# Causal attention of 4 batches: the row maxima of a batch are taken among the units of the batch before it

## The chip, the cores and the metric

One core of a Trainium2 chip runs the whole program, a decoder of several layers. The metric is the device time of one execution in microseconds; the median of three runs is given. The engines are TensorE (PE in the rows; PEld is its weight load), VectorE (DVE), ScalarE (ACT), GpSimd (POOL) and SyncE (SP). Each runs its own queue in order and waits on semaphores; only TensorE writes the eight banks of PSUM with matmuls, and VectorE and ScalarE read them.

## What is computed

The change lies in one of twelve layers, a causal self-attention over `x` of 4 batches (B) x 512 positions (S) x 128, with 16 heads of 8:

```python
q = split_heads(x @ Wq + bq)
k = split_heads(x @ Wk + bk)
v = split_heads(x @ Wv + bv)
att = jnp.einsum('bhtd,bhsd->bhts', q, k) * (1.0 / math.sqrt(Dh))
causal = jnp.tril(jnp.ones((T, T), dtype=bool))
att = jnp.where(causal[None, None], att, -jnp.inf)
att = jax.nn.softmax(att, axis=-1)
o = jnp.einsum('bhts,bhsd->bhtd', att, v)
o = o.transpose(0, 2, 1, 3).reshape(B, T, N_EMBD)
y = o @ Wo + bo
...
return (y - mu) * jax.lax.rsqrt(var + EPS) * gamma + beta
```

Its input is the layer-normed `x`, and its result is added to `x`. The softmax needs, for each query and head, a maximum that is subtracted before the exponential.

## The kernel before

The function `causal_attention` works in two passes over the scores. All data lies in SBUF; the stage issues no DMA.

**Looks** find the maxima. A look (`look(b, n)` on TensorE, `most(b, n)` on VectorE) covers one block of 128 queries against 128 or 256 keys, for 8 heads: it fills a pair of PSUM banks with 1024 columns of scores, and VectorE reduces them to 8 or 4 maxima per query (the line of `tensor_reduce` in `most`, L3328). A batch has LOOKS = 20. Looks with `kind == 0` lie on the diagonal: they first put a mask into both banks with an identity matmul of the whole 128 rows of the array (L3130), and then add the scores (L3134). These are the masked looks: numbers 0 to 3, 6, 7, 12 and 13 of a batch. Numbers 4, 5, 18, 19 (128 keys) and 8 to 11, 14 to 17 (256 keys) have no mask. The score matmuls of a look use 64 of the array's 128 rows, the lower or the upper half, by its `gp`, which alternates from look to look (even 0, odd 1).

When a batch's maxima are all there, TensorE turns them (`turn_most`, L3142) and VectorE subtracts them from the queries with four instructions (`shift`, L3337).

**Units** do the attention. A batch has UNITS = 16, `m` = 0 to 15; `c = m % 4` gives the first key block, so a unit covers 4, 3, 2 or 1 query blocks of 128 (512, 384, 256 or 128 columns). Unit `u` has two halves, `weigh(u, 0)` and `weigh(u, 1)` (L3154), each of which fills one pair of banks from one half of the array's rows. ScalarE takes the exponential of each half (L3302), GpSimd clears what lies above the diagonal (L3084), and three units later (LAG) TensorE multiplies with the values (`values`, L3168). After each 8 units the sums are copied, shifted (`shift_sums`, L3177), inverted on VectorE by a reciprocal (L3349), multiplied (L3351), and each batch is projected (`project_out`) and gets its bias.

**The order.** Each engine's order is written out by hand. Before, the loop over the looks of all four batches comes first (80 looks), with the projections of the next batch's q, k and v after looks 3 and 10 of a batch; then the loop over all 64 units. Six banks form a ring of three pairs, which is addressed with the running number of the look or of the half:

```python
both = lambda n: k.all_ps[:, 2 * (n % 3) * S:(2 * (n % 3) + 2) * S]
```

So a look waits for the reduction three looks before it, and a half for the exponential three halves before it. The seventh and eighth bank hold the sums over the values and everything else (projections, turned maxima, shifted sums).

Of the kernel before, what the change touches and what calls it, by code (L numbers as in the profile page):

```python
# [18 lines left out]
P = 128  # L19
# [3007 lines left out]
def causal_attention(nc, k, x, y, a):  # L3027
# [5 lines left out]
    GROUPS, UNITS, KEEP, LAG = 4, 16, 4, 3  # L3033
# [3 lines left out]
    LOOKS = len(looks)  # L3037
    names = ("consts zeroed q_ps q_out k_ps k_out v_ps v_out k_own k_own_late v_spread scores most m_ready m_turned q_shifted "
             "turned weights kept summed copied shifted inverted divided proj out "
             "centred squared var ln rooted y_ready sums_ln out_centred out_squared out_var out_ln out_rooted scaled done")  # L3040
    with ExitStack() as mem, stage(nc, names) as (block, s):
# [14 lines left out]
        both = lambda n: k.all_ps[:, 2 * (n % 3) * S:(2 * (n % 3) + 2) * S]  # L3056
# [33 lines left out]
        def _(pe):  # L3090
# [30 lines left out]
            def look(b, n):  # L3121
                i, kind, key, w, js, gp = looks[n]
                at = b * LOOKS + n
                after(pe, s["most"], at - 2)
                if at < 3:
                    pe.wait_ge(s["y_ready"], (2, 2, B)[at])
                    pe.wait_ge(s["ln"], (2, B, B)[at])
                if kind == 0:
                    for gl in range(2):
                        nc.tensor.matmul(both(at)[:, sl(gl)], k.ident_bf, later4[:, :], start=True, stop=False, skip_group_check=True)  # L3130
                for c, j in enumerate(js):
                    for gl in range(2):
                        rows = sl(2 * gp + gl, 32)
                        mm = nc.tensor.matmul(both(at)[:, gl * S + c * w:][:, 0:w], qj[b][rows, j * S + i * P:][:, 0:P], kd[b][rows, key:key + w],  # L3134
# [3 lines left out]
            def turn_most(b):  # L3138
                after(pe, s["divided"], 2 * b - 1)
# [5 lines left out]
            def weigh(u, p):  # L3145
                b, m = divmod(u, UNITS)
                j, c = divmod(m, TB)
                n, w = 2 * u + p, (TB - c) * P
                after(pe, s["weights"], n - 2)
                if n < 3:  # L3150
                    pe.wait_ge(s["most"], max(at for at in range(B * LOOKS) if at % 3 == n) + 1)
                for gl in range(2):
                    rows = sl(2 * p + gl, 32)
                    mm = nc.tensor.matmul(both(n)[:, gl * S:][:, 0:w], kj[b % 2][rows, j * S + c * P:][:, 0:P], qj[b][rows, j * S + c * P:][:, 0:w],  # L3154
# [3 lines left out]
            def values(u):  # L3158
# [6 lines left out]
                if m == 0:  # L3165
                    pe.wait_ge(s["v_spread"], b + 1)
# [147 lines left out]
        def _(dve):  # L3314
# [76 lines left out]
            for u in range(B * UNITS):  # L3391
# [4 lines left out]
                if b and m == 4:  # L3396
                    divide(2 * b - 1)
# [557 lines left out]
```

## Time and profile before

| what | us |
|---|---|
| median of 3 runs (1922.46 to 1943.81) | 1937.02 |
| the profiled execution | 1932.72 |
| its span | 1931.0 |
| looks, 1560.3 to 1678.1 | 117.8 |
| units, 1678.1 to 1804.5 | 126.4 |

The times of a view count from the start of the span. A timeline merges instructions of one kind that follow each other: its second column is the length of the merged piece, and x is their number. A matmul of float32 stands there as two records. The granted clock is TensorE's, as a share of 2.4 GHz. Over the whole span TensorE is busy 1700.8 us, VectorE 1150.9, ScalarE 961.8 and GpSimd 707.9; the stage in question is an eighth of the span, and the sections behind look at it alone.

### The profile page before, as it was taken

What the parts mean: (1) busy time and instruction counts of PE and PEld (TensorE: products, weight loads), DVE (VectorE), ACT (ScalarE), POOL (GpSimd) and SP (SyncE); (2) the same over time, 40 slices, a digit from 0 to 9 for tenths busy, and PEclk for the clock granted to TensorE, in tenths of its full rate; (3) what the DMA queues carried; (4) which work ended last, traced back from release to release, by engine and by line L of the source; (5) the groups of instructions that cost most, each with busy time, mean ns of one, the idle gap of its engine ahead of it and who ended that gap; (6) DMA issues with size and microseconds to landing.
All of it is one profiled execution on the core that took longest, in us unless ns stands there. A gap on an engine that the chain in (4) does not pass through costs nothing. (4 is left out here: it accounts for less than half of the span.)

```text
span 1931.0 us, 50165 instructions
## 1 busy us (share of the span) xinstructions
PE 1700.8 (88%) x19970; PEld 1190.9 (62%) x19970; DVE 1150.9 (60%) x2417; ACT 961.8 (50%) x2303; POOL 707.9 (37%) x947
## 2 busy tenths in 40 slices
PE   6884899785799999999999877899999999999885
PEld 4332899343457888888888743567986556533332
DVE  4444345359656777787775433666658867734434
ACT  4552444347586666666664344234543241166552
POOL 1103311306256767676674201572026510044201
PEclk9997899796799999999999889899999998899998
DMA  7311686000031000000000040424642200000100
GB/s 292 126 49 52 197 240 208 25 1 1 1 142 47 25 15 25 14 15 24 14 25 14 25 197 4 127 89 116 168 124 74 57 1 1 1 1 1 40 1 23
DMA packets 75641, 125.69 MB, mean 65 GB/s; under 512 B 10696, under 2 KB 55120, under 8 KB 73776
## 3 DMA queue, kind: packets, MB, share of 16 engines
q1 hardware_dynamic: 67408, 106.69, 17.2%
q0 software_dynamic: 6912, 15.61, 2.7%
q8 instruction: 165, 2.70, 0.6%
q14 instruction: 68, 0.56, 0.1%
q10 hardware_dynamic: 1088, 0.13, 0.0%
HBM read 83.73 MB, written 38.67 MB: 63 GB/s over the span
## 5 line engine op out<-in xcount | busy, mean ns | idle before, releaser
L2902 DVE SCALAR_TENSOR_TENSOR big<-bank,pack,big 128x256 f32<-128x256 f32 (+2 forms) x384 | 183.0, 478 | 41.9 <-ACT mask L2791 24.9
L2790 ACT ACTIVATE big<-bank,pack 128x256 f32<-128x256 f32 x192 | 90.8, 473 | 130.7 <-PE bank L2598 127.2
L2123 ACT ACTIVATE pack<-bank 128x512 f32<-128x512 f32 x96 | 57.5, 600 | 158.9 <-PE bank L785 95.2
L2508 POOL TENSOR_TENSOR big<-big,mask 128x256 f32<-128x256 f32 (+1 forms) x128 | 93.9, 733 | 91.1 <-DVE big L2902 57.5
L2585 PE MATMUL bank<-big 128*128 128x128 f32 x896 | 124.0, 286 | 1.5 <-issue 1.3
L2598 PE MATMUL bank<-y,pack 128*128 128x262 f32 (+1 forms) x384 | 120.9, 400 | 4.9 <-DVE big L2902 4.6
L3302 ACT ACTIVATE pt<-bank 128x1024 f32<-128x1024 f32 (+3 forms) x128 | 79.6, 705 | 89.6 <-PE bank L3154 89.6
L783 PE MATMUL bank<-yh,wl 128*128 128x512 f32 x192 | 112.9, 588 | 11.6 <-DVE a L2283 6.8
L1921 POOL DMA_INDIRECT pack<-results,where x64 | 67.4, 1053 | 150.9 <-PE bank L1992 136.7
L3084 POOL TENSOR_SCALAR_AFFINE_SELECT pt<-pt 128x256 f32<-128x256 f32 x128 | 55.2, 443 | 166.1 <-ACT pt L3302 163.8
L2585 PEld LDWEIGHTS bank<-big 128*128 128x128 f32 x896 | 108.0, 192 | 6.9 <-issue 3.0
L3328 DVE TENSOR_REDUCE part<-bank 128x8 f32<-128x1024 f32 (+1 forms) x80 | 93.6, 1218 | 15.7 <-PE bank L3134 14.8
L1154 DVE SCALAR_TENSOR_TENSOR a<-bank,big,a 128x128 f32<-128x128 f32 x184 | 51.8, 344 | 81.8 <-ACT a L1066 71.9
L1992 PE MATMUL bank<-a,big 128*128 128x512 f32 x192 | 99.0, 599 | 1.0 <-DVE a L2283 1.0
L2277 DVE TENSOR_TENSOR pack<-pack 128x512 f32<-128x512 f32 x90 | 62.4, 693 | 49.5 <-ACT pack L2123 31.8
L3134 PE MATMUL bank<-big 32*128 32x128 f32 (+1 forms) x1024 | 85.0, 325 | 4.1 <-DVE part L3328 4.1
L3134 PEld LDWEIGHTS bank<-big 32*128 32x128 f32 x1024 | 66.8, 197 | 31.6 <-issue 16.9
L1066 ACT ACTIVATE a<-bank,big 128x128 f32<-128x128 f32 x184 | 52.6, 368 | 58.7 <-PE bank L963 50.4
L785 PE MATMUL bank<-yh,wh 128*128 128x512 f32 x192 | 76.6, 399 | 0.0
L2968 DVE COPY_PREDICATED t<-level_masks,bank 128x256 f32<-128x256 uint8 x64 | 28.6, 446 | 80.1 <-PE bank L2589 80.1
L784 PE MATMUL bank<-yl,wh 128*128 128x512 f32 x192 | 76.0, 396 | 0.0
L1914 POOL DMA_INDIRECT wide_sorted<-y,where x64 | 66.3, 1036 | 26.3 <-issue 16.6
(665 smaller groups left out, 4451.1 us busy)
## 6 DMA issues: line engine op xcount, KB each, us to landing
big<-in_experts SPq DMA_DIRECT2D x46, 516.0 KB
big<-in_big SPq DMA_DIRECT2D x1, 9216.0 KB, 26.1
gate<-big SPq DMA_DIRECT2D x32, 256.0 KB
z<-gate SPq DMA_DIRECT2D x16, 512.0 KB
pack<-routing SPq DMA_DIRECT2D x60, 128.0 KB
wide_sorted<-big SPq DMA_DIRECT2D x5, 1472.0 KB, 13.0
pack<-in_pack SPq DMA_DIRECT2D x1, 5910.5 KB, 20.8
pack<-wide_sorted SPq DMA_DIRECT2D x16, 256.0 KB, 3.2
```

Source lines behind the costliest of these rows:

```text
L783: nc.tensor.matmul(out, pl, dh[:, cur], start=start, stop=False)
L784: nc.tensor.matmul(out, ph, dl[:, cur], start=False, stop=False)
L785: return nc.tensor.matmul(out, ph, dh[:, cur], start=False, stop=stop)
L1992: nc.tensor.matmul(sums(n), down_block(n // 2), h(n), start=n < 2, stop=n >= N - 2).then_inc(s["down"], 1)
L2508: nc.gpsimd.tensor_tensor(d, d, tap_of(i)[:, :, c:], ALU.add).then_inc(s["whole"], 1)
L2585: mm4 = lambda out, gr, left_, right: [nc.tensor.matmul(out[:, sl(h % GH, P)], left_(h), right(h), start=True, stop=True) for h in hs(gr)][-1]
L2598: nc.tensor.matmul(haloed(i)[:, :, 3 - halo:], k.w["L2_attn_qkv_w"][:, sl(m, P)], tokens, start=True, stop=True).then_inc(s["raw"], 1)
L2790: nc.scalar.activation(dst3(i), conv_in(i, 0), ACT.Copy, scale=weight(i, 3))
L2902: ins = nc.vector.scalar_tensor_tensor(out=d, in0=conv_in(i, back), scalar=weight(i, 3 - back), in1=d, op0=ALU.mult, op1=ALU.add)
L3134: mm = nc.tensor.matmul(both(at)[:, gl * S + c * w:][:, 0:w], qj[b][rows, j * S + i * P:][:, 0:P], kd[b][rows, key:key + w], start=kind != ...
L3302: nc.scalar.activation(dst, src, ACT.Exp, scale=-1.0).then_inc(s["weights"], 1)
L3328: nc.vector.tensor_reduce(dst, src, AX.X, ALU.max).then_inc(s["most"], 1)
```

## The change

Only the first batch's 20 looks, and the first four (AHEAD) of batch 1, stay in front of the units. The other 56 go among the units of the batch in front of theirs, by a table: units of four blocks get none, the others none to two.

```diff
+    per_unit = [(0, 1, 2, 2) * 3 + (0, 1, 0, 0)] + [(0, 2, 2, 2) + (0, 1, 2, 2) * 2 + (0, 2, 2, 0)] * 2
+
+    def looks_by(b, m):
+        return (b + 1) * LOOKS + (AHEAD if b == 0 else 0) + sum(per_unit[b][:m])
+
+    def looks_in(u):
+        b, m = divmod(u, UNITS)
+        return range(looks_by(b, m), looks_by(b, m + 1)) if b + 1 < B and m + 1 < UNITS else range(0)
+
+    ring = [("most", at) for at in range(LOOKS + AHEAD)]
+    for u in range(B * UNITS):
+        more = list(looks_in(u))
+        ring += [("weights", 2 * u)] + [("most", at) for at in more[:-1]] + [("weights", 2 * u + 1)] + [("most", at) for at in more[-1:]]
+    place = {item: i for i, item in enumerate(ring)}
...
+            def reuse(i):
+                if i >= 3:
+                    name, n = ring[i - 3]
+                    pe.wait_ge(s[name], n + 1)
```

The ring of three bank pairs now counts looks and halves together in the order of TensorE (`place`), and each waits for the reader of the pair three places before (`reuse`). On TensorE the two loops become:

```diff
-            for b in range(B):
-                pe.wait_ge(s["k_out"], b + 1)
-                for n in range(LOOKS):
-                    look(b, n)
-                    if b + 1 < B and n == 3:
-                        project_qk(b + 1)
-                    if b + 1 < B and n == 10:
-                        project_v(b + 1)
-                    if b == B - 1 and n == LOOKS - 7:
-                        turn_most(0)
+            for at in range(LOOKS):
+                look(at)
+                if at in (1, 7, 13):
+                    project_qk(at // 6 + 1)
+                if at in (5, 11, 17):
+                    project_v(at // 6 + 1)
+            look(LOOKS)
+            turn_most(0)
+            for at in range(LOOKS + 1, LOOKS + AHEAD):
+                look(at)
...
                     weigh(u, 0)
+                    for at in looks_in(u)[:-1]:
+                        look(at)
                     weigh(u, 1)
+                    for at in looks_in(u)[-1:]:
+                        look(at)
```

VectorE takes the reductions of a unit's looks before its other work of that unit. All three later projections of q, k and v move into the 20 looks of batch 0. The inverses of the sums move from VectorE to ScalarE, and the products on VectorE move a unit or two back:

```diff
+                if b and m == 5:
+                    invert_sums(2 * b - 1)
+                if m == 13:
+                    invert_sums(2 * b)
...
             def divide(half):
-                dve.wait_ge(s["shifted"], half + 1)
-                if half < LAST:
-                    after(dve, s["proj"], half // 2)
-                    nc.vector.reciprocal(o[half % 2], k.ps[7]).then_inc(s["inverted"], 1)
                 dve.wait_ge(s["inverted"], half + 1)
                 nc.vector.tensor_tensor(o[half % 2], raw[half % 2], o[half % 2], ALU.mult).then_inc(s["divided"], 1)
...
-                if b and m == 4:
+                if b and m == 6:
                     divide(2 * b - 1)
-                if b and m == 9:
+                if b and m == 10:
                     add_bias(b - 1)
-                if b < B and m == 12:
+                if m == 14:
                     divide(2 * b)
```

`invert_sums` is a logarithm and an exponential of -1 times it.

The order on TensorE in the first units of batch 0 (L3154 before and L3176 after are the halves, L3168 and L3191 the values, L3153 the masks and L3157 the scores of looks). Before:

```order
L3154 MATMUL bank<-big 128x384 x4
L3154 MATMUL bank<-big 128x256 x4
L3154 MATMUL bank<-big 128x128 x4
L3168 MATMUL bank<-pt,vj 32x512 x4
L3154 MATMUL bank<-big 128x512 x4
```

After:

```order
L3157 MATMUL bank<-big 128x128 x8
L3176 MATMUL bank<-big 128x256 x2
L3157 MATMUL bank<-big 128x128 x8
L3176 MATMUL bank<-big 128x256 x2
L3153 MATMUL bank<-later_28447,ident_bf 128x512 x2
L3157 MATMUL bank<-big 128x128 x8
L3176 MATMUL bank<-big 128x128 x2
L3153 MATMUL bank<-later_28447,ident_bf 128x512 x2
L3157 MATMUL bank<-big 128x128 x8
L3176 MATMUL bank<-big 128x128 x2
L3157 MATMUL bank<-big 128x256 x4
L3191 MATMUL bank<-pt,vj 32x512 x4
```

The four matmuls of a unit are split into two and two, with a look between them and one behind them.

The order on VectorE from the last reductions of batch 1's queries on, at the seam of batches 0 and 1 (L3392 copies sums, L3379 multiplies with the inverse, L3369 shifts the queries). Before (L3364 the copy, L3349 the reciprocal, L3351 the product, L3337 the shift), where no reductions are left:

```order
L3364 COPY big<-bank 128x512
L3349 RECIPROCAL big<-bank 128x512
L3351 TENSOR_TENSOR big<-big 128x512
L3337 SCALAR_TENSOR_TENSOR big<-bank,pack,big 128x512 x4
L3364 COPY big<-bank 128x512
```

After:

```order
L3360 TENSOR_REDUCE part<-bank 128x2x2 x3
L3392 COPY big<-bank 128x512
L3360 TENSOR_REDUCE part<-bank 128x2x2
L3360 TENSOR_REDUCE part<-bank 128x8 x2
L3363 TENSOR_REDUCE big<-part 128x16
L3379 TENSOR_TENSOR big<-big 128x512
L3369 SCALAR_TENSOR_TENSOR big<-bank,pack,big 128x512 x4
L3360 TENSOR_REDUCE part<-bank 128x8 x2
```

The reciprocal is gone, and reductions of the next batch stand around each piece of the units' work.

## Rows read from the trace of the kernel before

**Rows 1.** Stretches: length, busy us of PE, PEld, DVE, ACT, POOL, granted clock.
```profile
1560.30:1678.10 117.80, 112.91 (x1132) 76.42 (x1131) 100.81 (x105) 17.85 (x27) 1.49 (x4) 0.92 0.01 1
1678.10:1804.50 126.40, 122.63 (x1063) 47.18 (x1063) 48.99 (x46) 79.63 (x128) 56.55 (x132) 0.95 0.00 1
1587.20:1604.30 17.10, 17.10 (x94) 10.10 (x92) 7.76 (x9) 2.72 (x5) 0.00 (x0) 0.50 0.00 1
...
1675.90:1689.60 13.70, 13.26 (x72) 6.27 (x72) 3.38 (x4) 5.86 (x9) 3.17 (x8) 0.50 0.00 0
```

**Rows 2.** Groups by shape, 1545 to 1835: busy us, mean ns | idle before, releaser.
```profile
L3328 DVE TENSOR_REDUCE part<-bank 128x8 f32<-128x1024 f32 x48 | 57.3, 1219 | 15.3 <-PE bank L3134 14.5
...
L3302 ACT ACTIVATE pt<-bank 128x768 f32<-128x768 f32 x32 | 24.3, 814 | 5.3 <-PE bank L3154 5.3
L3349 DVE RECIPROCAL big<-bank 128x512 f32<-128x512 f32 x7 | 23.5, 3358 | 29.0 <-PE bank L3177 29.0
...
L3302 ACT ACTIVATE pt<-bank 128x256 f32<-128x256 f32 x32 | 10.7, 384 | 0.0
```

**Rows 3.** Timeline of PE, 1561.9 to 1570.5: start us, us, what; full clock.
```profile
1563.60 0.60 PE L3130 MATMUL bank<-later,ident_bf 128*128 128x512 bf16 x2
...
1565.23 0.60 PE L3130 MATMUL bank<-later,ident_bf 128*128 128x512 bf16 x2
...
1566.85 1.12 PE L3111 MATMUL bank<-y,pack 128*128 128x512 f32 x2
...
1568.77 1.72 PE L3134 MATMUL bank<-big 32*128 32x128 f32 x32
1570.42 0.39 PE L3130 MATMUL bank<-later,ident_bf 128*128 128x512 bf16 x1
```

**Rows 4.** Timeline of PE, 1575 to 1579, full clock.
```profile
1576.13 1.16 PE L3118 MATMUL bank<-pack,y 128*128 128x128 f32 x8
1577.22 1.13 PE L3134 MATMUL bank<-big 32*128 32x256 f32 x8
1578.29 0.61 PE L3130 MATMUL bank<-later,ident_bf 128*128 128x512 bf16 x2
```

**Rows 5.** Timeline of DVE, 1581.6 to 1589.
```profile
1581.66 8.01 DVE L3328 TENSOR_REDUCE part<-bank 128x8 f32<-128x1024 f32 x7
```

**Rows 6.** Timeline of PE, 1590 to 1598, clock at half.
```profile
1590.55 1.03 PE L3130 MATMUL bank<-later,ident_bf 128*128 128x512 bf16 x2
...
1593.53 1.03 PE L3130 MATMUL bank<-later,ident_bf 128*128 128x512 bf16 x2
```

**Rows 7.** Timeline of PE, 1677 to 1804.5: the first unit of batches 1 and 2.
```profile
1710.12 1.14 PE L3154 MATMUL bank<-big 32*128 32x512 f32 x8 [0.84 <-DVE big L3337]
...
1741.63 1.14 PE L3154 MATMUL bank<-big 32*128 32x512 f32 x8 [0.84 <-DVE big L3337]
```

**Rows 8.** Timeline of all engines, 1748.4 to 1757: units of batch 2.
```profile
1748.41 1.14 PE L3154 MATMUL bank<-big 32*128 32x512 f32 x8
...
1749.59 1.94 ACT L3302 ACTIVATE pt<-bank 128x1024 f32<-128x1024 f32 x2 [1.90 <-PE bank L3154]
...
1750.26 1.13 PE L3177 MATMUL bank<-big,pack 128*128 128x512 f32 x2
...
1751.32 0.93 PE L3154 MATMUL bank<-big 32*128 32x384 f32 x8
...
1752.18 0.64 PE L3168 MATMUL bank<-pt,vj 128*32 128x256 f32 x8
...
1754.13 0.69 PE L3154 MATMUL bank<-big 32*128 32x128 f32 x8
...
1754.76 1.07 PE L3168 MATMUL bank<-pt,vj 128*32 128x512 f32 x8
...
1755.75 1.14 PE L3154 MATMUL bank<-big 32*128 32x512 f32 x8
```

**Rows 9.** Timeline of ACT, 1806 to 1808: the logarithm of the last half's sums.
```profile
1806.49 0.60 ACT L3259 ACTIVATE big<-bank 128x512 f32<-128x512 f32 x1 [0.29 <-PE bank L3177]
```

More of the change, by code:

```diff
@@ L3055, in causal_attention @@
         LAST = 2 * B - 1
-        both = lambda n: k.all_ps[:, 2 * (n % 3) * S:(2 * (n % 3) + 2) * S]
+        both = lambda i: k.all_ps[:, 2 * (i % 3) * S:(2 * (i % 3) + 2) * S]
         @block.gpsimd
@@ L3119, in project_v, with look @@
                 mm.then_inc(s["v_ps"], 1)
-            def look(b, n):
+            def reuse(i):
+                if i >= 3:
+                    name, n = ring[i - 3]
+                    pe.wait_ge(s[name], n + 1)
+            def look(at):
+                b, n = divmod(at, LOOKS)
                 i, kind, key, w, js, gp = looks[n]
-                at = b * LOOKS + n
-                after(pe, s["most"], at - 2)
+                dst = both(place["most", at])
+                reuse(place["most", at])
                 if at < 3:
@@ L3127, in look @@
                     pe.wait_ge(s["ln"], (2, B, B)[at])
+                if n == 0:
+                    pe.wait_ge(s["k_out"], b + 1)
                 if kind == 0:
                     for gl in range(2):
-                        nc.tensor.matmul(both(at)[:, sl(gl)], k.ident_bf, later4[:, :], start=True, stop=False, skip_group_check=True)
+                        nc.tensor.matmul(dst[:, sl(gl)], k.ident_bf, later4[:, :], start=True, stop=False, skip_group_check=True)
                 for c, j in enumerate(js):
@@ L3147, in weigh @@
                 j, c = divmod(m, TB)
[L3148 to L3151, printed above, removed]
+                i, w = place["weights", 2 * u + p], (TB - c) * P
+                reuse(i)
                 for gl in range(2):
                     rows = sl(2 * p + gl, 32)
-                    mm = nc.tensor.matmul(both(n)[:, gl * S:][:, 0:w], kj[b % 2][rows, j * S + c * P:][:, 0:P], qj[b][rows, j * S + c * P:][:, 0:w],
+                    mm = nc.tensor.matmul(both(i)[:, gl * S:][:, 0:w], kj[b % 2][rows, j * S + c * P:][:, 0:P], qj[b][rows, j * S + c * P:][:, 0:w],
                                           start=True, stop=True, tile_position=(rows.start, 0))
@@ L3259, in invert_sums @@
                 nc.scalar.activation(o[half % 2], k.ps[7], ACT.Ln).then_inc(s["sums_ln"], 1)
[L3260 removed]
+                act.wait_ge(s["sums_ln"], half + 1)
                 nc.scalar.activation(o[half % 2], o[half % 2], ACT.Exp, scale=-1.0).then_inc(s["inverted"], 1)
@@ L3318, in add_rows, with most @@
                                         k.w["L3_attn_bv"].unsqueeze(1).broadcast_to([P, TB, P]), ALU.add).then_inc(s["v_out"], 1)
-            def most(b, n):
+            def most(at):
+                b, n = divmod(at, LOOKS)
                 i, kind, key, w, js, gp = looks[n]
-                at = b * LOOKS + n
-                src = both(at).rearrange("p (g j w) -> p g j w", g=2, w=w)
+                src = both(place["most", at]).rearrange("p (g j w) -> p g j w", g=2, w=w)
                 first = (i * 3 + kind) * H + gp * 8 + js[1]
@@ L3383, in _ @@
             dve.wait_ge(s["zeroed"], 4 + B)
-            for b in range(B):
-                for n in range(LOOKS):
-                    most(b, n)
-                    if b + 1 < B and n == 11:
-                        add_rows(b + 1)
-                    if b == B - 1 and n == LOOKS - 5:
-                        shift(0)
+            for at in range(LOOKS + 1):
+                most(at)
+                if at in (6, 12, 18):
+                    add_rows(at // 6)
+            shift(0)
+            for at in range(LOOKS + 1, LOOKS + AHEAD):
+                most(at)
             for u in range(B * UNITS):
```

12 lines of the change are left out of this document (8 added, 4 removed).

## Prediction

> **What bounds the kernel now.** I read the table of stretches first, for the two parts of this stage that the change joins. The maxima of all four batches take 117.8 us, the 64 units after them 126.4 us [rows 1]. In the maxima VectorE works 100.8 us; in the units it works 49.0 us, of which 23.5 us are seven reciprocals of 3.36 us [rows 1, 2]. So VectorE looks like the bound of the first part and idle in the second, and the change brings its work there.
>
> Whether that pays depends on TensorE, which both parts need. Its timeline shows three paces. A look with masked blocks (8 of a batch's 20) issues two identity matmuls on the whole array and then sixteen short ones on half of it: 1.63 us from one to the next (1563.60 to 1565.23) [rows 3], more than VectorE's 1.22 us for its reduction [rows 2]. A look without mask takes 1.07 us (1577.22 to 1578.29) [rows 4], and two in a row, on the two halves of the array, 1.65 us for both (1568.77 to 1570.42) [rows 3]. There VectorE sets the pace: seven reductions in 8.01 us, so (8.01 - 1.22) / 6 = 1.13 us each [rows 5]. At the lower level of the clock (1.2 GHz; 2.4 is the other) the masked look takes 2.98 us (1590.55 to 1593.53) [rows 6]. The granted clock was 0.50 for 17.1 us of the maxima and for 13.7 us at the seam to the units; the means of the two parts, 0.92 and 0.95, leave full clock for the rest [rows 1].
>
> In the units TensorE is nearly the bound. Four units take 6.78 us (1741.63 to 1748.41), sixteen, a batch, 31.5 us (1710.12 to 1741.63) [rows 7, 8]. The next four take 7.34 us with a shift of sums of 1.06 (1750.26 to 1751.32) among them, so 6.28 without it [rows 8]: at least 0.5 us of the 6.78 is waiting, 2.0 us a batch. ScalarE works 79.6 us of 126.4 [rows 1]. A unit's two halves run side by side: eight matmuls of 512 columns take 1.14 us, as long as eight of 256 in a look, which has half the array [rows 4, 8]. This is the catch: VectorE has room in the units, TensorE has little, and what a look costs there is TensorE time.
>
> **The maxima before the units.** 24 looks are left, 12 of them masked, with all three later projections among them. TensorE: 12 x 1.63 = 19.6; six pairs x 1.65 = 9.9; three projections of q and k at 1.92 (1566.85 to 1568.77) = 5.8; three of v at 1.09 (1576.13 to 1577.22) = 3.3; the turn about 0.6, half a projection of v; together 39.2 us [rows 3, 4]. VectorE would need 24 x 1.13 = 27 plus some 6 for added rows and the shift: TensorE is the bound. Two waits are new: a projection of q and k waits for added rows that stand behind a reduction (0.3 us, twice), and the turn after look 20 waits for the last reduction of batch 0 (about 1.2, one reduction). I take 41.1 us, if the clock stays full; 39 and 43 are the bounds. The units begin 117.8 - 41.1 = **76.7 us** earlier.
>
> **The units.** 56 looks come in: 16 during batch 0, 20 each during batches 1 and 2. By kind, what each adds to its unit:
> - masked pair: the identity matmuls take the whole array, so nothing runs beside them, and only the unit's second half can hide beside a look: 2 x 1.63 = 3.3 us.
> - masked single, after both halves: 1.63. Single without mask: 1.07.
> - pair without mask: the ring of three double banks decides. The second look gets the banks of the unit's own first half and waits for that exponential. At three blocks: scores 0.93, exponential 0.81, two hand-overs of 0.05 (1748.41 + 1.14 to ScalarE's 1749.59), the look 1.07, together 2.91, less the unit's own 0.86 (1751.32 to 1752.18): 2.05. At one block 0.69 + 0.38 + 0.10 + 1.07 - 0.63 = 1.6. At two blocks between them, 1.8 [rows 2, 4, 8].
> - mixed pair: between 1.63 (the look without mask hidden) and 2.70 (nothing hidden); I take 2.5, as each look shares its half of the array with one of the unit's own.
>
> Batch 0: one masked pair, two mixed, three without mask (two, two and one blocks), four singles: 3.3 + 5.0 + 5.2 + 4.3 = 17.8. Batches 1 and 2: three masked pairs, one masked single, one mixed, five without mask (three, two and three times one block), one single: 9.8 + 1.6 + 2.5 + 8.7 + 1.1 = 23.7 each. Sum 65.2. Against it stand the waits of now, since a longer unit need not wait for its exponential. Some come back: a unit's first half gets the banks of a look, whose reduction may be 1.13 us behind another. Of the 2.0 us a batch I take 1.5 as won, 4.5 in all, between 0 and 6. The units grow by **60.7 us**.
>
> The seven reciprocals go to ScalarE as a logarithm (0.60 us, as the last half has it already [rows 9]) and an exponential of about the same: 8.4 us on an engine with over 40 us idle, which hides them. Without that cover the exponentials behind, and the second look's wait with them, move by 1.2 us, seven times. On VectorE some 33 us a batch (25 for looks, 8 of its own) stand in 54. Bias, shift and late keys are queued behind at most two reductions of 1.22, and TensorE asks for them a unit or more later, the shift of queries excepted: it stands where it stood, after unit 15, which has no look. No DMA is touched.
>
> **The sum.** 76.7 - 60.7 = 16.0 us gained, with the clock of the units as it was. The old first part lost to the low clock about four masked looks x 1.35 and a projection's 1.8, 7 us [rows 3, 6]; the first batch of units some 3.5: it took 32.0 us from 1678.1, and has 3.0 less of its own (a shift of 1.06 and a projection of about 1.9) than the 31.5 of the later ones [rows 1, 7]. If the new stage stays at full clock all along it gains 16.0 + 3.5 = 19.5; if it loses as much as the old, 16.0 - 7 = 9. I take 15. The profiled execution had 1932.7 us (its span 1931.0): 1917.7 for it. The median of the runs is 4.3 above: 1937.0 - 15 = **1922.0 us**.
>
> **Rivals.**
> - *Better overlap.* Rows 3 and 8 show both halves of the array at work together. If looks without mask never waited at the ring, ten or eleven pairs and the mixed ones would add about 1.07, 11 us less, and with full clock 4 more: 1937 - 30 = 1907. Against it: the ring has three places whatever the order.
> - *No overlap.* Half-array pieces of looks and units run one after the other. A unit whose halves are split then pays its scores twice, 0.63 to 0.86 in 20 units, 15 us: 1937, no change. Rows 8 speak against it, since the halves do run together; but there they stand side by side in the queue.
> - *The other side: the clock.* Before it fell at 1587.2 TensorE ran looks at VectorE's pace, with short waits between them [rows 1, 5]; the merged units have many such waits, at banks that two engines hand back. A masked look takes 1.82 times as long at the low level [rows 3, 6], so each us spent there loses 0.45. Some 33 us beyond my allowance take the gain; 76, half of the 152 us of merged units, make it slower by 1%: 1956. Against it: the clock was full in most of both parts, with the same kind of waits [rows 1].
>
> The Trainium skill has a rule for this last one ("TensorE: Matmul & The Clock Gate", "A second HAM failure mode: psum-queue depth-cycling"): a TensorE that cycles through PSUM banks and idles briefly between groups of matmuls swings between both levels. This trace agrees with it in 30.8 us of 244 only. If it held for half of the merged units, the time would be the 1956 us of that rival.
>
> **How the numbers follow.** My forecast has 0.62 (its own range 1914 to 1931), better overlap 0.14, no overlap 0.14, the clock 0.10. The time is that of the likeliest, 1922.0. The range goes from 1905, the first rival and a little, to 1940, the second and the clock's first 35 us. About 1% (19.4 us) is what a measurement of this kernel tells from no change. Faster by more: the first rival, and a fifth of my own case, full clock all along: 0.27. Slower by more: the worse half of the clock case: 0.06. Within 1%: 0.67.
>
> **What would show it.** The first unit's scores start 41 us after 1560.3 (45 or more: low clock, or a projection that waits). Batch 0 of the units takes about 45 us, 1 and 2 take 53 to 54, batch 3 takes 31. Loads of looks' weights wait for exponentials, about a dozen times. Masked looks add 1.6 in the units too. VectorE has no reciprocal left. I am wrong in the units if batches 1 and 2 take 48 (overlap) or 60 (none), and in the clock if the merged units' granted clock is under 0.9.

## The result, and the profile after

The changed kernel takes 1916.49 us (median of 20 runs, 1908.18 to 1928.87) where the kernel before takes 1934.47 beside it (20 runs). The two medians lie 18.0 us apart. The ratio of the fast runs alone, without the few clearly longer ones, is 0.9941, with a 95% interval from 0.9919 to 0.9963: between 7 and 16 us less, most likely 11. The two measures differ by over 6 us, so the whole time tells the gain only roughly. Forecast were 15 us and 1922.0. The profiled execution of the changed kernel has 1909.3 us, below its median.

The spans of the two profiled executions, before first, with the mean granted clock:

```profile
core 0: 1931.0 us, clock 0.938
```

```profile
core 0: 1907.6 us, clock 0.950
```

They lie 23.4 us apart, but the changed stage gives only part of that. It took 244.2 us before and takes 228.2 now, 15.9 less. The other 7.5 us lie in code that the change does not touch. In both executions TensorE spent time at the lower level of its clock elsewhere too: 209 us outside the stage before, 194 after. In the profiles of the experiments this number lies anywhere from 183 to 217. So the stage is where kernels are to be compared, and I give its length for each.

The stage after, by stretches (length, busy us of PE, PEld, DVE, ACT, POOL, granted clock): the looks ahead, then the units of batches 0 to 3. They answer to [rows 1]. The last row ends 1.2 us before the last values.

```profile
1549.40:1589.60 40.20, 37.29 (x381) 25.24 (x381) 32.79 (x37) 17.71 (x27) 1.48 (x4) 1.00 0.01 1
1589.60:1634.60 45.00, 43.67 (x451) 22.72 (x449) 24.28 (x26) 22.11 (x34) 12.94 (x32) 1.00 0.01 1
1634.60:1689.30 54.70, 52.94 (x540) 27.32 (x540) 32.06 (x38) 23.78 (x36) 14.78 (x34) 1.00 0.01 2
1689.30:1744.00 54.70, 52.95 (x540) 27.33 (x540) 32.07 (x38) 23.78 (x36) 14.78 (x34) 1.00 0.00 1
1744.00:1776.50 32.50, 30.42 (x268) 11.49 (x272) 5.38 (x8) 22.04 (x36) 12.63 (x32) 1.00 0.01 1
```

TensorE works 53 of 54.7 us in a batch with 20 looks in it, VectorE 32. And the clock is full in every stretch, where [rows 1] has 17.1 and 13.7 us at half. The groups by shape, 1535 to 1805 (busy us, mean ns | idle before, releaser):

```profile
L3360 DVE TENSOR_REDUCE part<-bank 128x8 f32<-128x1024 f32 x48 | 57.9, 1221 | 44.0 <-PE bank L3157 43.9
...
L3288 ACT ACTIVATE big<-big 128x512 f32<-128x512 f32 x8 | 5.0, 630 | 0.3
L3286 ACT ACTIVATE big<-bank 128x512 f32<-128x512 f32 x8 | 4.8, 601 | 0.3 <-PE bank L3200 0.3
```

A reduction takes 1221 ns, as in [rows 2], but VectorE now idles 44.0 us before them, and always for the looks' scores on TensorE; before it was 15.3. The roles have changed over. The inverses are 601 + 630 ns on ScalarE.

One unit shows how it runs now: TensorE and ScalarE in unit 1 of batch 2, a unit of three blocks that has two masked looks (L3176 halves, L3153 masks, L3157 looks' scores, L3191 values, L3330 exponentials).

```profile
1691.16 0.92 PE L3176 MATMUL bank<-big 32*128 32x384 f32 x4
...
1692.01 0.60 PE L3153 MATMUL bank<-later,ident_bf 128*128 128x512 bf16 x2
...
1692.55 0.82 PE L3157 MATMUL bank<-big 32*128 32x128 f32 x10
1693.11 0.59 PE L3176 MATMUL bank<-big 32*128 32x384 f32 x2
...
1693.21 0.50 PE L3157 MATMUL bank<-big 32*128 32x128 f32 x6
...
1693.53 0.49 PE L3176 MATMUL bank<-big 32*128 32x384 f32 x2
...
1693.95 0.61 PE L3153 MATMUL bank<-later,ident_bf 128*128 128x512 bf16 x2
...
1694.07 0.81 ACT L3330 ACTIVATE pt<-bank 128x768 f32<-128x768 f32 x1 [0.94 <-PE bank L3176]
1694.49 0.97 PEld L3157 LDWEIGHTS bank<-big 32*128 32x128 f32 x16 [0.42 <-issue]
1694.49 1.16 PE L3157 MATMUL bank<-big 32*128 32x128 f32 x16
...
1695.58 0.64 PE L3191 MATMUL bank<-pt,vj 128*32 128x256 f32 x8
```

From 1691.16 to 1695.58 there is no gap. The first half runs alone, the masks run alone, and the second half runs between pieces of the first look's scores (1693.11 to 1693.53), as the other half of the array is free for it. The second masked look runs alone: 1.63 us (1693.95 to 1695.58). Scores and looks take 4.42 us, where the same unit of before took 0.86 for its scores.

### The profile page after: what moved, and what is told of

The parts are those of the page before. It is cut to its first block and busy times, and to the rows that moved or that the text cites. A ratio compares the mean times of both kernels' runs of the same rounds, so it can differ in the third digit from the quotient of the medians.

```text
span 1907.6 us, 50177 instructions
## 1 busy us (share of the span) xinstructions
PE 1676.2 (88%) x19970; PEld 1176.4 (62%) x19970; DVE 1127.0 (59%) x2410; ACT 971.7 (51%) x2317; POOL 706.5 (37%) x947
## 5 line engine op out<-in xcount | busy, mean ns | idle before, releaser
L3330 ACT ACTIVATE pt<-bank 128x1024 f32<-128x1024 f32 (+3 forms) x128 | 84.2, 704 | 105.8 <-PE bank L3176 105.6
L3157 PE MATMUL bank<-big 32*128 32x128 f32 (+1 forms) x1024 | 84.1, 308 | 1.2 <-DVE part L3360 0.9
L3157 PEld LDWEIGHTS bank<-big 32*128 32x128 f32 x1024 | 66.1, 186 | 24.0 <-issue 15.1
L3176 PE MATMUL bank<-big 32*128 32x128 f32 (+3 forms) x512 | 73.7, 477 | 5.2 <-DVE big L3369 2.5
L1914 POOL DMA_INDIRECT wide_sorted<-y,where x64 | 67.2, 1051 | 26.8 <-issue 13.9
```

The lines of the kernel that those rows point to most:

```text
L3157: mm = nc.tensor.matmul(dst[:, gl * S + c * w:][:, 0:w], qj[b][rows, j * S + i * P:][:, 0:P], kd[b][rows, key:key + w], start=kind != 0, s ...
L3176: mm = nc.tensor.matmul(both(i)[:, gl * S:][:, 0:w], kj[b % 2][rows, j * S + c * P:][:, 0:P], qj[b][rows, j * S + c * P:][:, 0:w], start=T ...
L3330: nc.scalar.activation(dst, src, ACT.Exp, scale=-1.0).then_inc(s["weights"], 1)
```

## The experiments

Two theories stood against each other on most runs, named A and B in the texts on record. Stage lengths are from the first look to the last values; a batch's length goes from its first unit to the next batch's. Every kernel was measured beside the kernel before on the same chip. Numbers 5 to 8 and 11 are one execution each, so for them it is the stage that is compared, and the whole time says little.

**1. The kernel before once more.** No edit.

> The kernel before once more, with nothing edited, for the granted clock of its executions beside those of the changed kernel (0.937 to 0.950 in 20 runs). The profile of before had 30.8 us at half clock inside the two stretches that the change joins, that of the changed kernel none up to the end of the units. Theory A, the clock is chance and the merged units get no more and no less than the old parts did: a mean clock like that of the changed kernel, less what the 16 us of saved span explain, 0.940 to 0.946; the stage in this profile has anything from 0 to 35 us at half clock. Theory B, the looks at VectorE's pace bring the clock down and the merged units keep it up: mean clock 0.934 to 0.939, and 17 to 31 us at half clock in the looks again. Time ratio to before 1.00 in both.

1911.55 us against 1916.88, ratio 0.9968 (0.9934 to 1.0003). Looks 117.2, units 126.1, stage 243.2, and again 17.1 and 13.7 us at half clock in the same two places of the stage. The one at the seam of looks and units begins 2.2 and 3.5 us before the units; the one among the looks begins 26.8 and 25.0 us behind the first look. So both came back, but number 4 will show that the order of the instructions alone does not fix the one among the looks. The mean clock over the span, 0.932 to 0.950 over the runs of before and this one, does not tell the kernels apart, since most of the cold time lies in other layers.

**2. Both looks behind both halves.**

```diff
                     weigh(u, 0)
-                    for at in looks_in(u)[:-1]:
-                        look(at)
                     weigh(u, 1)
-                    for at in looks_in(u)[-1:]:
+                    for at in looks_in(u):
                         look(at)
```

> The changed kernel with both looks of a unit behind its two halves, in place of one between them; the ring is counted in that order. Theory A (the ring and TensorE decide, and a look between the halves keeps the second half back): a masked pair's unit of three blocks goes from 4.42 to about 0.86 + 2 x 1.63 + 0.1 = 4.2 us, two blocks from 3.99 to 3.95, pairs without mask stay at 2.9 and 2.5 since the second look waits for the same exponential; a batch 1 to 2 us shorter, the kernel 2 to 5 us, ratio to before 0.992. Theory B (a half that runs beside a look on the other half of the array is what makes looks cheap): every unit with two looks pays its scores once more, 0.6 to 0.9 us in 20 units, 13 to 16 us longer, ratio 1.001.

1914.46 us, ratio 0.9983 (0.9952 to 1.0014), same chip as 1. Batches 1 and 2 take 55.8 instead of 54.7: one microsecond more, where A expected less and B at least five more (0.6 to 0.9 in each of nine units). Some units lose (unit 15: 3.98 for 3.51, unit 7: 3.73 for 3.20), some win (unit 6: 3.34 for 3.66, unit 9: 4.50 for 4.86). Both theories miss: splitting the halves is worth 1.1 us a batch, no more. Batch 0 took 53.9 instead of 45.0, with the clock at half for 13.7 us of it:

```profile
1589.80:1603.40 13.60, 12.36 (x83) 6.57 (x86) 5.00 (x5) 0.80 (x3) 1.00 (x3) 0.50 0.00 1
```

So merged units can fall to half clock as well. Of the 8.9 us that batch 0 grew, 7.0 lie in its units 2 to 4, where the stretch is; the rest is spread over later units at full clock.

**3. The reciprocals back on VectorE**, in the changed kernel; products and bias at their old units.

```diff
-                if b and m == 5:
-                    invert_sums(2 * b - 1)
-                if m == 13:
-                    invert_sums(2 * b)
...
             def divide(half):
+                dve.wait_ge(s["shifted"], half + 1)
+                if half < LAST:
+                    after(dve, s["proj"], half // 2)
+                    nc.vector.reciprocal(o[half % 2], k.ps[7]).then_inc(s["inverted"], 1)
                 dve.wait_ge(s["inverted"], half + 1)
```

> The changed kernel with the seven inverses as reciprocals on VectorE again, at the old places (products after units 4 and 12, bias after 9). In batch 3 no look stands behind them: the two waits of 1.15 us at units 7 and 15 of that batch go, 2.3 us won. Theory A (a reduction behind 3.36 us of reciprocal comes late and holds a bank pair): units 5, 6, 13 and 14 of batches 0 to 2 grow by 1 to 1.5 us at each of five places, 5 to 7 us lost, so 3 to 5 us slower than the changed kernel, ratio to before 0.996. Theory B (VectorE has room enough): no unit of batches 0 to 2 grows, and the kernel is 2.3 us faster than the changed one, ratio 0.993.

1919.22 us, ratio 1.0004 (0.9970 to 1.0038): no gain over before is left. The stage takes 243.2, 15 more than the changed kernel's; A expected 3 to 5. The timeline of VectorE and of TensorE in batch 1, and the stretches of low clock in batches 1 and 2:

```profile
1679.57 3.36 DVE L3377 RECIPROCAL big<-bank 128x512 f32<-128x512 f32 x1 [2.49 <-PE bank L3200]
1682.96 0.69 DVE L3379 TENSOR_TENSOR big<-big 128x512 f32<-128x512 f32 x1
1683.57 2.35 DVE L3356 TENSOR_REDUCE part<-bank 128x4 f32<-128x1024 f32 x2
```

```profile
1684.84 1.22 PE L3176 MATMUL bank<-big 32*128 32x256 f32 x4 [1.85 <-DVE part L3356]
```

```profile
1684.70:1698.40 13.70, 12.72 (x86) 6.82 (x88) 6.60 (x9) 3.40 (x6) 1.99 (x5) 0.50 0.00 1
1746.20:1759.90 13.70, 12.62 (x88) 6.72 (x89) 6.70 (x9) 3.30 (x6) 1.94 (x5) 0.50 0.00 1
```

Two reductions are queued behind the reciprocal and its product, and end at 1685.92 (1683.57 + 2.35); TensorE needs the first one's banks and waits 1.85 us. Right there the clock falls, for 13.7 us. The second stretch begins 61.5 us later, one batch, at the same unit. Units 13 and 14 take 5.38 and 5.32 for 3.46 and 2.92, unit 15 and the first of the next batch 4.57 and 3.46 for 3.51 and 1.85: together 7.0 us a batch. Batch 0 has a shorter stretch at its end (6.8 us) and is 2.1 us longer. Units 5 to 7, which have a reciprocal too, are as long as ever (3.06, 3.75, 3.11). So the reciprocal costs little by itself. The stall of 1.85 us and the half clock that comes with it stand for most of the 15 us; no run separates the two.

**4. The inverses alone**: the kernel before, with `invert_sums` on ScalarE after units 5 and 13 as in the change, and nothing else of it.

```diff
+                if b and m == 5:
+                    invert_sums(2 * b - 1)
+                if m == 13:
+                    invert_sums(2 * b)
...
-                    nc.vector.reciprocal(o[half % 2], k.ps[7]).then_inc(s["inverted"], 1)
```

> The kernel before with one part of the change alone: the inverses of the sums on ScalarE, products after units 6 and 14, bias after unit 10; all looks stay in front. Theory A (without looks beside them the exponentials behind the inverse come late, as in the last batch of the changed kernel, 1.15 us at units 7 and 15): seven such places, 8 us slower than before, ratio 1.004. Theory B (those two waits in the last batch come from something else in the changed order): no unit grows, ratio 1.000.

1924.26 us, ratio 1.0028 (0.9989 to 1.0066). Each unit 7 and 15 behind such an inverse is 1.15 us longer (2.77 for 1.62, 4.27 for 3.12), in all seven places, 8.05 us, as A had it. ScalarE around one of them:

```profile
1730.93 0.60 ACT L3259 ACTIVATE big<-bank 128x512 f32<-128x512 f32 x1
1731.56 0.63 ACT L3261 ACTIVATE big<-big 128x512 f32<-128x512 f32 x1
1732.10 1.61 ACT L3303 ACTIVATE pt<-bank 128x512 f32<-128x512 f32 x4
```

The next exponentials stand behind the two, and TensorE's short units wait for them. The looks of this kernel had no cold stretch: 109.8 us, where before has 117.7 with 17.1 cold. So a cold stretch among the looks costs 7.9 us, and it doesn't always come: the looks of numbers 1 and 4 are issued in the same order, and up to the place where number 1 falls, 25.0 us behind the first look, TensorE's waits of over 0.1 us stand at the same places in both (the longest 0.20 us) and agree within 4 ns. Number 1's stretch, and the same one in number 4:

```profile
1567.80:1584.80 17.00, 16.34 (x105) 11.38 (x104) 9.41 (x10) 0.21 (x1) 0.00 (x0) 0.50 0.00 1
```

```profile
1567.10:1584.10 17.00, 16.20 (x190) 11.43 (x192) 14.45 (x16) 3.36 (x5) 0.00 (x0) 1.00 0.00 1
```

What made the difference is open. The stretch at the seam is there in number 4 as well, 13.7 us long. Less its seven waits the stage of number 4 would be 236.2 us: 8.0 over the changed kernel's, where the profile of before is 15.9 over it.

**5 and 6. No masked looks**: the identity matmuls are left out, in the kernel before (5) and in the changed one (6). The same edit in both:

```diff
-                if kind == 0:
+                if kind < 0:
                     for gl in range(2):
```

> The kernel before without the identity matmuls that mask the blocks on the diagonal; the maxima then run over later keys too, so this part of the computation is left out. Each of 32 masked looks took TensorE 1.63 us at full clock. Theory A (VectorE paces every look that has no mask, one per 1.13 us): the looks of before fall from 117.7 us (of it some 7 lost to half clock) to 80 x 1.13 plus some 9 of added rows, merges and shift, 99 to 102 us at full clock, up to 110 with a stretch at half. Theory B (TensorE still decides, since it also has the projections): 110 us or more at full clock. Units unchanged, 31.5 us a batch.

> The changed kernel without the identity matmuls that mask the blocks on the diagonal (that part of the computation is left out). Theory A (in the merged units every us of TensorE counts, and a pair without mask costs what the ring lets through): unit 1 of batch 1 falls from 4.99 to about 3.4 us, unit 2 from 4.34 to 2.9, unit 5 from 3.05 to 2.5, unit 10 from 4.35 to 2.9; a batch from 54.7 to 48 to 49 us. The 24 looks ahead of the units become bound by VectorE: 40.2 to 34 to 35 us. Theory B (the merged units are held by the ring and by VectorE, 28 reductions and 5 other operations, not by TensorE's matmuls): a batch stays above 53 us.

On one chip, one execution each: before 1905.82, number 5 1909.0, number 6 1896.42. Number 5 has the masks of 32 looks less to pay, and its stage is only 4.4 us shorter than before's (239.8), its looks take 113.0 us, over A's 99 to 110. Three stretches of it:

```profile
1562.60:1576.30 13.70, 13.70 (x122) 11.16 (x120) 12.31 (x13) 0.74 (x2) 0.00 (x0) 0.50 0.01 1
1576.30:1583.10 6.80, 6.37 (x84) 4.68 (x84) 5.12 (x6) 2.62 (x5) 0.00 (x0) 1.00 0.00 0
1583.10:1596.80 13.70, 13.70 (x102) 11.28 (x104) 11.08 (x12) 0.00 (x0) 0.00 (x0) 0.50 0.01 1
```

The clock swings between its levels, and in six stretches TensorE is at half clock for 75 us of the stage, 63 of them in the looks. In the two cold rows TensorE is busy all of the 13.70 us and VectorE 12.31 and 11.08: at half clock TensorE is the slower of the two even without masks. None of my theories had that much half clock.

The Trainium skill ("TensorE: Matmul & The Clock Gate", "A second HAM failure mode: psum-queue depth-cycling") tells of a TensorE that goes through PSUM banks, idles briefly between groups and swings between the two levels. The trace of number 5 agrees, with its 75 us; that of the changed kernel doesn't, with 188 us of units at full clock.

In number 6 the units with masked looks lose nearly what A expected: unit 1 3.67 for 4.99 (two masks: 1.32 us less), unit 2 2.92, unit 5 2.31 for 3.05, and batches 1 and 2 49.5 for 54.7 (A: 48 to 49). A mask costs about 0.7 us of TensorE in a merged unit; its two matmuls take 0.54 (1692.01 to 1692.55 above). The looks ahead take 39.7, not the 34 to 35 expected: TensorE waits 3.1 us in them for the added rows and 2.1 for the maxima that it turns, and 6.5 us are at half clock. Batch 0 takes 48.2 for 45.0, as a stretch of 20.5 us at half clock from 1581.3 lies mostly in it.

**7 and 11. Reductions over half the columns**, in the changed kernel (7) and in the kernel before (11). VectorE reads 512 of 1024 columns, so that its maxima cover half the keys.

```diff
-                nc.vector.tensor_reduce(dst, src, AX.X, ALU.max).then_inc(s["most"], 1)
+                nc.vector.tensor_reduce(dst, src[:, :, :, 0:w // 2], AX.X, ALU.max).then_inc(s["most"], 1)
```

> The changed kernel with reductions over half of each row's columns (1.22 us become about 0.68; the maxima over the other half are left out). Theory A (TensorE is the bound and VectorE's speed only matters where a bank pair comes back late, 8 us of such waits in the whole stage): the looks ahead of the units lose 2 to 3 of 40.2 us, batches 1 and 2 of the units lose at most 1.5 us of 54.7, and stay above 53. Theory B (the reductions hold the ring): 20 of them a batch, 0.54 us shorter each, so a batch falls by 5 to 10 us, to 45 to 50.

> The kernel before with reductions over half of each row's columns (the maxima over the other half are left out). Theory A (VectorE paced the looks without mask, TensorE the masked ones): per batch 8 x 1.63 + 6 x 1.65 + 3.0 of projections = 26 us, so the 80 looks fall from 117.7 to 102 to 106 us at full clock. Theory B (TensorE paced all of them already): 110 us or more at full clock. If waiting for VectorE is what lowers the clock, at most 14 us of the looks stand at half clock, in place of 20.

Number 7: 1893.23 us beside a before of 1905.82. Its batches take 52.9 for 54.7, its looks ahead 36.9 for 40.2, the stage 220.6: 7.6 us less, at full clock. With a reduction of 0.69 us in place of 1.22, a merged batch gets 1.8 us shorter, a little more than A's 1.5 and far from B's 5 to 10: TensorE bounds it.

Number 11: 1910.0 us beside a before of 1928.81. Its looks take 97.7 us, 20.0 less than before and under A's 102 to 106, its stage 223.6. The two rows are its looks and the start of its units; it has no other cold stretch.

```profile
1554.60:1652.00 97.40, 92.95 (x1112) 67.76 (x1126) 60.91 (x104) 17.55 (x26) 1.48 (x4) 1.00 0.01 2
1652.00:1662.20 10.20, 10.13 (x52) 4.75 (x48) 1.02 (x3) 5.12 (x8) 3.20 (x8) 0.50 0.00 0
```

This pair tells where the change's gain comes from. With full reductions the stage is 15.9 us shorter after the change (8.0 where the looks stay at full clock, as in number 4); with halved ones 3.0 (223.6 to 220.6), and number 11 still has 10.2 us cold. So when VectorE is not the pace of the looks, moving them among the units brings next to nothing.

**8. Masked looks in pairs**: the masks of two looks first, then their scores together, one look on each half of the array; the pair stands behind both halves of its unit.

```diff
+                for e in range(2):
+                    reuse(place["most", at + e])
+                    for gl in range(2):
+                        nc.tensor.matmul(dsts[e][:, sl(gl)], k.ident_bf, later4[:, :], start=True, stop=False, skip_group_check=True)
+                for c, j in enumerate(js):
+                    for e in range(2):
+                        for gl in range(2):
...
```

> The changed kernel with masked looks in pairs: where a unit, or the part ahead of the units, has two masked looks in a row of which the first uses the lower half of the array, both masks are put down first, and then the scores of both looks are issued alternately, so that the halves of the array work together; in such a unit both looks stand behind both halves of the unit. Theory A (a masked look costs 1.63 us because nothing runs beside it; 2 x 0.54 for the masks and 1.15 for both scores is what a pair needs): four pairs ahead of the units lose 0.8 us each, down to VectorE's 2.44, so 40.2 becomes 37; in the units a pair loses 0.3 to 0.9 us in its own unit and gives some of it back in the next, where a half waits for the first reduction, batches 1 and 2 at 53 to 54 us. Theory B (the scores of two looks don't run together when they are issued alternately): 40 us ahead of the units and 56 or more in a batch.

1907.15 us beside 1905.82. The pairing itself works, 32 records of two looks in 1.17 us, but the next unit pays (TensorE in batch 2):

```profile
1692.92 1.17 PE L3186 MATMUL bank<-big 32*128 32x128 f32 x32
...
1696.76 0.81 PE L3181 MATMUL bank<-later,ident_bf 128*128 128x512 bf16 x3 [0.66 <-DVE part L3399]
...
1699.99 1.16 PE L3164 MATMUL bank<-big 32*128 32x128 f32 x16 [0.54 <-DVE part L3399]
```

Unit 1 is 0.76 us shorter (4.23) and unit 10 0.96 (3.39), unit 3 1.1 longer (4.47) and unit 11 as well (4.64): both looks of a pair end together, so their reductions come one after the other behind it, and the ring of three waits for them. Batches 1 and 2 take 56.7 and 55.3, where A had 53 to 54 and B 56 or more, and the looks ahead grow to 42.4 where 37 were expected; 3.4 us of these and 3.4 of batch 1 are at half clock. What A took for a saving is a loan.

**9. The changed kernel once more, and 10, two repairs together**: the two inverses that ScalarE takes during batch 3's units as reciprocals on VectorE, and the turn of batch 0's maxima one look later.

```diff
             look(LOOKS)
+            look(LOOKS + 1)
             turn_most(0)
-            for at in range(LOOKS + 1, LOOKS + AHEAD):
+            for at in range(LOOKS + 2, LOOKS + AHEAD):
...
-                if b and m == 5:
+                if b and b < B - 1 and m == 5:
                     invert_sums(2 * b - 1)
-                if m == 13:
+                if b < B - 1 and m == 13:
                     invert_sums(2 * b)
```

> The changed kernel once more, with nothing edited, to stand beside the next run on the same chip and for a second profile. Theory A (the merged units keep TensorE's clock up): at most 14 us at half clock between the first look and the last values, and batches 1 and 2 of the units at 54.7 us again; stage 228 to 232 us. Theory B (the clean profile was luck): 20 us or more at half clock in the stage, 235 us or more. Ratio to before 0.990 to 0.997 with A.

> The changed kernel with two repairs: in batch 3, where no look covers them, the two inverses are reciprocals on VectorE as in the kernel before (products after units 4 and 12); and the turned maxima of batch 0 come after look 21 in place of 20, so that TensorE need not wait for the last reduction of batch 0. Theory A (both waits are TensorE's own and nothing fills them later): units 7 and 15 of batch 3 lose 1.15 us each, 33.7 becomes 31.4 us; the looks ahead of the units lose 1.2 us of 40.2, as VectorE has that much room there. 3.5 us faster than the changed kernel, ratio to before 0.992 where the changed kernel has 0.994. Theory B (the waits move): the front stays at 40 us since VectorE's shift now comes later and unit 0 waits for it; 2.3 us faster at most.

Beside a before of 1928.81, number 9 takes 1915.82, ratio 0.9933 (0.9899 to 0.9968), and number 10 1917.18, ratio 0.9945 (0.9909 to 0.9981). Number 9 repeats the stage to 0.3 us: 228.0, batches 44.95, 54.72, 54.72, 33.67, no cold stretch. Number 10 does what both repairs are for, batch 3 31.4 for 33.7 and looks ahead 38.6 for 40.2, and loses it in batch 0, which takes 53.1 for 45.0. TensorE at its first unit, and the stretches around:

```profile
1598.15 2.06 PE L3176 MATMUL bank<-big 32*128 32x512 f32 x12 [1.45 <-DVE part L3361]
```

```profile
1595.60:1600.10 4.50, 3.05 (x28) 1.00 (x24) 3.63 (x5) 1.79 (x2) 0.41 (x1) 1.00 0.00 0
1600.10:1617.20 17.10, 16.57 (x115) 9.85 (x116) 6.31 (x6) 4.04 (x8) 2.85 (x7) 0.50 0.00 1
```

The later turn pushes the shift of batch 0's queries, and with it a reduction that the unit's second half waits for, 1.45 us. Behind that wait the clock is at half for 17.1 us, and the stage takes 232.6. I did not run the two repairs apart, so whether the inverses of batch 3 alone would beat the changed kernel by their 2.3 us is open; it is less than a comparison here resolves.

## Why the prediction was right, and where it was not

**What bounds the two parts.** Right, and numbers 7 and 11 show it, with one profile each. The looks of before had both bounds: at full clock 109.8 us (number 4), and 97.7 with halved reductions, so VectorE's pace cost 12.1. In the merged stage it costs 7.6. TensorE is what the units run at.

**The front: 41.1 us forecast, 40.2 measured.** Batch 0's looks with all projections fit in as worked out. 1.2 us of it is TensorE waiting for the maxima that it turns:

```profile
PE bank L3166 <- DVE big L3363: 1.2, 1, 1.2
```

**The units: +60.7 forecast, +61.6 measured.** The terms by unit, batch 1, after less before:

| looks | forecast | measured |
|---|---|---|
| masked pair, units 1, 2, 10 | 3.3 each | 3.18, 3.15, 3.35 |
| masked single, unit 5 | 1.63 | 1.62 |
| mixed pair, unit 6 | 2.5 | 2.28 |
| unmasked pair, three blocks, unit 13 | 2.05 | 2.02 |
| unmasked pair, two blocks, unit 14 | 1.8 | 1.54 |
| unmasked pair, one block, units 3, 7, 11 | 1.6 each | 1.42, 1.58, 1.55 |
| unmasked single, unit 9 | 1.07 | 1.13 |
| unit 15, no look | 0 | 0.39 |
| batch | 23.7, less 1.5 won | 23.2 |

The two rates of the array, alone under a mask and side by side otherwise, carried over from the looks to the merged units. The credit of 1.5 us a batch for waits won back was wrong: growth stands only 0.5 under the sum of the terms, so 1.0 of the credit is missing in each of batches 1 and 2. The weight loads still wait for exponentials and reductions in the merged stage:

```profile
PEld bank L3176 <- DVE part L3360: 5.4, 12, 0.9
...
PEld bank L3157 <- ACT pt L3330: 4.8, 10, 0.8
PEld bank L3176 <- ACT pt L3330: 4.8, 7, 1.1
```

Ten loads of looks' scores wait for an exponential and, by the same view, two of masks: the dozen forecast. The twelve waits of halves for a reduction are what took the credit: in number 7, with halved reductions, one of 0.8 us is left of these 5.4, and a batch is 1.8 us shorter.

**The inverses: forecast nothing, measured 2.3 us.** This step failed in batch 3. The prediction gave ScalarE's idle time as the cover, and 1.2 us each as the price without it. Idle time of an engine is no cover when it lies elsewhere; in batch 3 there is no look in the unit, so nothing of TensorE's lies between the late exponential and the half that waits. ScalarE and TensorE there:

```profile
1756.08 0.60 ACT L3286 ACTIVATE big<-bank 128x512 f32<-128x512 f32 x1
...
1756.72 0.63 ACT L3288 ACTIVATE big<-big 128x512 f32<-128x512 f32 x1
1757.26 1.61 ACT L3330 ACTIVATE pt<-bank 128x512 f32<-128x512 f32 x4
...
1757.89 0.49 PE L3176 MATMUL bank<-big 32*128 32x128 f32 x4 [0.86 <-ACT pt L3330]
```

Twice 1.15 us, so batch 3 takes 33.7 instead of the 31 forecast. In batches 1 and 2 the looks do cover unit 7's inverse (+1.58 with its pair, forecast 1.6); unit 15 has no look, and its 0.39 is not the inverse's: TensorE waits there 0.54 us for VectorE's product with it, ahead of the turned maxima, and with halved reductions that wait is gone (2.93 us for 3.51). The product is queued behind reductions, a term that the prediction left out. Number 4 had the same 1.15 in seven places, and number 3 shows that the move was worth making all the same.

**The sum, and the clock.** 15.9 us were won in the stage, by the working 16.0 "with the clock of the units as it was". That agreement is partly luck. The clock was not as it was: the new stage is at full clock throughout, for which the prediction had 19.5. The 3.6 us short are the inverses in batch 3 (2.3), the missing credit in batches 1 and 2 (2.0) and 0.2 in batch 0, less 0.9 from the front. I took 15 between 19.5 and 9 without knowing which clock would come.

Seen by cause, the 15.9 us between the two profiles are mostly clock. Before, the cold stretch in the looks cost 7.9 us (number 4) and the one at the seam about 3.5 (batch 0 took 32.0, and 31.5 less the 3.0 that it lacks is 28.5; this is worked out, no run of before had a warm seam). So of 15.9 us some 11.4 are half-clock time that is gone and 4.5 are the better division of VectorE's work, which is just 12.1 less 7.6. The two parts of the clock are not equally firm. The stretch at the seam is in all five profiles that keep the looks ahead (before and numbers 1, 4, 5 and 11). The one among the looks is in two of the three with whole looks (before and number 1, not 4). Where it stays away the change wins about 8 us in the stage, not 16.

**The rivals.** Better overlap (pairs at 1.07, batches of 48) did not come: 54.7. No overlap (batches of 60) neither. The clock rival's mechanism exists, though not in the changed kernel's profiles: numbers 2, 3 and 10 are small edits of it, and each has 13.7 to 34.1 us at half clock in the stage; number 6 has 23.9. Each microsecond there costs 0.4 to 0.5: 7.0 of 13.7 in number 2, 7.9 of 17.1 in the looks of before, and 6.9 of 17.1 in number 10 (batch 0 is 8.2 us longer, 1.3 of them in unit 0, ahead of the stretch). The prediction took 0.45. The sentence that the clock fell when TensorE "ran looks at VectorE's pace, with short waits" fits number 5 well. It is not enough: the looks of number 4 run at the same pace, with the waits of number 1, and don't fall. And at the seam of before, and in numbers 3 and 10, a single longer wait stands ahead of the fall. Before, at the seam:

```profile
1675.73 1.92 PE L3134 MATMUL bank<-big 32*128 32x128 f32 x16 [2.60 <-DVE part L3328]
```

Yet the wait of 1.20 us ahead of the turned maxima in the changed kernel has no fall behind it, and in number 2, which has the same wait, the fall came 11 us later, behind waits of 0.19 and 0.38. So what decides stays open. Shown is that some places repeat: the seam of before in every profile, the two stretches of number 3 one batch apart, and none in the two profiles of the changed kernel (its own and number 9); and that one among the looks does not always.

**The whole time.** The ratio says 11.4 us, number 9's 12.9, the medians 18.0; the stage says 15.9 against the profile of before and 8.0 against number 4's looks. A kernel before whose looks fall to half clock in some executions and not in others would lie between the last two. That is not shown, since only profiled executions tell where the clock was low. What is shown is a gain, and that the agreement of 15.9 with the forecast is closer than the measurement is sharp.

**Smaller slips of the working.** The terms of the front add up to 41.0, not 41.1. The better-overlap rival counts ten or eleven pairs, while the prediction's own list has thirteen without a mask and four mixed, which at 1.07 would give 14 us and not 11. And where it says sixteen or eight matmuls it counts records, two to a matmul.

## What to carry to other kernels

Before work is moved among other work, ask what of the two engines' time is really exclusive: here only 4.5 of the 15.9 us came from the better division of work, the rest was half-clock time of the old order, and the moved work cost TensorE as much as it had cost ahead. Before time at half clock is counted as won, see whether it comes back in a second profile: the larger of the two stretches was missing in one of three. Price moved work by the rates it has alone and beside the other half of the array, and give no credit for waits that a ring of buffers may take again. An engine's idle time covers an added instruction only if it lies between the same two hand-overs: look at the unit where it lands, the ones without the change's other work too.

## What the hardware showed unexpectedly

- Leaving out 64 identity matmuls of the kernel before made its looks only 4.7 us shorter (117.7 to 113.0), as TensorE then spent 75 us of the stage at half clock, for 30.8 before.
- Two executions with the looks in the same order, and with TensorE's waits equal within 4 ns for 25.0 us, parted there: one went to half clock for 17.1 us, the other did not.
- A wait of 1.85 us of TensorE recurred with a stretch of 13.7 us at half clock in two batches, 61.5 us apart; each batch was 7.0 us longer, far more than the wait.
- Matmuls of a look and of a unit's second half, on different halves of the array, run interleaved piece by piece, though one stands wholly ahead of the other in the queue (1693.11 to 1693.53): the overlap came without an order that alternates them.
- Two masked looks with their scores paired take 1.17 us for 32 records (16 matmuls), as long as 16 records alone (1.16).
